# A graph network's edge rows: scattered to turns with one two-block row each, gathered once in the score pass, second blocks at the end of the last pass

## The reference, cut to what matters

```python
def _L0_gnn_ref(h, src, dst, W1, b1, W2, b2, eps):      # 3 layers
    for l in range(3):
        agg = segment_sum(h[src], dst, n)
        z = (1.0 + eps[l]) * h + agg
        h = maximum(z @ W1[l] + b1[l], 0.0) @ W2[l] + b2[l]
    return h
def _L1_gnn_ref(h, w, a, src, dst):
    hi, hj = h[src], h[dst]
    e = leaky_relu(concatenate([hi, hj], -1) @ w, 0.2) @ a
    exp_e = exp(e)
    att = exp_e / segment_sum(exp_e, src, N)[src]
    return segment_sum(hi * att, dst, N)
x = layernorm(x + _L0_gnn_ref(x, ...))
x = layernorm(x + _L1_gnn_ref(x, ...))
```

## Time and profile before

| what | value |
|---|---|
| time, median of 3 | 11068.61 us (11064.67 to 11077.53) |
| span of the profiled execution, first to last instruction | 9426.8 us |
| its own time beyond the span | not given by the page |
| POOL / PE / DVE / ACT busy | 7036.3 / 6946.3 / 5337.9 / 4916.2 us |
| layer 0, 78 to 2016 us | 1938 us |
| score stage, first gather to the last pass's first load | 2123.37 us |
| last pass, to its last turn | 1068.02 us |

### The profile page before, as it was taken

One profiled execution on the slowest core, in us unless ns is written; L12 is line 12 of the kernel. 1 busy time (PEld: TensorE's weight loads), 2 busy tenths in 40 slices (PEclk: granted clock), 3 DMA queues, 4 the chain that ended last, 5 costly groups with the idle time before them and its releaser, 6 DMA issues.

```text
span 9426.8 us, 148122 instructions
## 1 busy us (share of the span) xinstructions
PE 6946.3 (74%) x27727; PEld 4824.0 (51%) x27728; DVE 5337.9 (57%) x18200; ACT 4916.2 (52%) x11010; POOL 7036.3 (75%) x7500
## 2 busy tenths in 40 slices
PE   6777777777777777777777777777767777777776
PEld 4444444444444444444444444566667667666665
DVE  4444444444444444444444444567777777778888
ACT  5555555555555555565555555422222222267777
POOL 6777777767777777767777777667777777778886
PEclk7666666676666666676656666778887787889998
DMA  3222222232222222222222222366666666645554
GB/s 93 53 53 53 53 53 53 53 78 53 53 53 53 53 53 53 53 75 53 53 53 53 53 53 53 91 173 182 182 180 181 182 181 181 182 136 139 140 140 133
DMA packets 937711, 898.45 MB, mean 95 GB/s; under 512 B 258861, under 2 KB 778726, under 8 KB 937635
## 3 DMA queue, kind: packets, MB, share of 16 engines
q0 software_dynamic: 244544, 529.59, 21.8%
q1 hardware_dynamic: 627697, 265.87, 10.1%
q10 hardware_dynamic: 65426, 102.51, 4.0%
HBM read 751.91 MB, written 143.82 MB: 95 GB/s over the span
## 4 chain that ended last, share of the span: by engine, by line
POOL 63%; issue 23%; DVE 7%; PE 2%; ACT 2%; DVEq 1%; POOLq 1%; DMA 1%; ACTq 0%; SPq 0%
POOL rows L755 54%; POOL work L755 6%; DVE agg L1549 4%; POOL hot L755 2%; DVE big L1783 2%; ACT hot L1035 1%; PE psum L1291 1%; PE psum L1166 0%; POOLq L767 0%; ACT work L1072 0%; POOLq L459 0%; DVEq L1783 0%; PE psum L1180 0%; PE psum L1158 0%; PE psum L1189 0%
## 5 line engine op out<-in xcount | busy, mean ns | idle before, releaser
L1158 PE MATMUL psum<-work,rows 128*128 128x256 f32 x9408 | 4306.2, 607 | 1522.8 <-DMA rows<-table_g,idx_now 1000.8
L1563 DVE TENSOR_TENSOR agg<-agg,psum 128x128 f32 x9408 | 2703.0, 287 | 3152.6 <-PE psum L1158 2840.1
L1158 PEld LDWEIGHTS psum<-work,rows 128*128 128x128 f32 x9408 | 2504.6, 293 | 3323.5 <-issue 1204.5
L755 POOL DMA_INDIRECT rows<-table_g,idx_now x3136 | 2968.9, 947 | 1022.1 <-issue 1021.2
L920 ACT ACTIVATE work<-big,one_col 128x1024 f32<-128x1024 f32 x1176 | 1348.3, 1147 | 2354.3 <-PE psum L1158 2351.3
L912 ACT ACTIVATE big<-iota_w,rel_now 128x256 f32<-128x256 f32 x4704 | 1971.6, 495 | 51.9
L755 POOL DMA_INDIRECT rows<-in_x,idx_now x1568 | 1483.0, 946 | 523.3 <-issue 523.3
L996 ACT ACTIVATE work<-psum 128x256 f32<-128x256 f32 x832 | 320.7, 385 | 1456.5 <-PE psum L1256 1445.1
L755 POOL DMA_INDIRECT rows<-table_p,idx_now x832 | 803.3, 966 | 265.9 <-issue 265.3
L1291 PE MATMUL psum<-rows,hot 128*128 128x128 f32 x3328 | 658.8, 326 | 228.3 <-ACT hot L1035 201.2
L1252 PE MATMUL psum<-big,work 128*128 x3328 | 778.5, 321 | 47.4 <-ACT work L997 33.3
(11 more groups left out here) (194 smaller groups left out, 5447.2 us busy)
## 6 DMA issues: line engine op xcount, KB each, us to landing
rows<-x_of SPq DMA_DIRECT2D x416, 256.0 KB, 2.9
work<-rel_rows ACTq DMA_DIRECT2D x208, 256.0 KB
x_of<-rows SPq DMA_DIRECT2D x208, 256.0 KB, 4.2
rows<-table_g,idx_now POOLq DMA_INDIRECT x3136, 2.5
x_of<-work SPq DMA_DIRECT2D x156, 256.0 KB
big<-lo_rows ACTq DMA_DIRECT2D x208, 192.0 KB
rows<-in_x,idx_now POOLq DMA_INDIRECT x1568, 2.5
rows<-table_p,idx_now POOLq DMA_INDIRECT x832
```

The source lines that it names most:

```text
L755: pool.indirect_dma_start(out=to, out_offset=None, in_=table, in_offset=bass.IndirectOffsetOnAxis(ap=idx_now[:, at:at + 1], axis=0)) \
L1158: ins = pe.matmul(sums_at(q, t % QUAD), ring[:, t, :], span_hot[q][:, t % QUAD, :], start=True, stop=True)
L1563: dve.tensor_tensor(to, to, sums_at(q, j)[:, k * P:(k + 1) * P], ALU.add).then_inc(added[a], 1)
```

## The change

The layers' rows, in the order in which they are, are now written to new places instead of being read again. After layer 0, POOL scatters the prologue's `src` rows (`placed_src`) and relative-`dst` rows with both block numbers (`placed_rel`) to DRAM, 26 indirect DMAs with indices `place_i`, which a rank of the two-block rows gives: each turn's first place takes one two-block row, the other 15 places take one-block rows. SP loads them back, and DVE and PE go on as before. The score pass then has 98 turns (`T2` = 1568 rows) rather than 104: each row is gathered once, and the first row of a turn gets a second matmul for its second block (`hot_second`, made by DVE from the same `rel_row`). The last pass still has 104 turns: the first 1564 (`REAL`) rows, then the second blocks of the turns' first rows, whose features SP reads from `x1_of` a second time, at every 16th row.

```diff
@@ gpsimd @@
-            def gather_edges(table, to, landed):
+            def place_rows(table, of):
                 for r in range(RG):
-                    pool.indirect_dma_start(out=to[:, r, :], out_offset=None, in_=table,
-                                            in_offset=bass.IndirectOffsetOnAxis(ap=row_i[:, r:r + 1], axis=0)) \
-                        .then_inc(landed, 16)
+                    pool.indirect_dma_start(out=table, out_offset=bass.IndirectOffsetOnAxis(ap=place_i[:, r:r + 1], axis=0),
+                                            in_=of[:, r, :], in_offset=None).then_inc(rows_placed, 16)
...
-                with pool.Fori(0, LAPS if no == LAYER_A else LAPS2) as i:
+                with pool.Fori(0, LAPS2) as i:
...
@@ sync, after layer 0's tables @@
+            sp.wait_ge(rows_placed, 2 * 16 * RG)
+            sp.dma_start(g_srcf, placed_src.rearrange("(r p) e -> p r e", p=P)).then_inc(src_in, 16)
+            sp.dma_start(g_relw, placed_rel.rearrange("(r p) e -> p r e", p=P)).then_inc(dst_in, 16)
...
+            sp.dma_start(lo_all.rearrange("(r p) e -> p r e", p=P), g_lo16).then_inc(lo_out, 16)
+            sp.wait_ge(lo_out, 16)
+            sp.dma_start(lo_rows[0:REAL, :], lo_all[0:REAL, :]).then_inc(lo_out, 16)
+            sp.dma_start(lo_rows[REAL:T, :], lo_all[0:SECONDS * TPI, :].rearrange("(k s) e -> k s e", s=TPI)[:, 0, :]).then_inc(lo_out, 16)
@@ sync, last pass @@
+            def load_seconds(at, first, n):
+                sp.dma_start(slots[:, at:at + n, 0:D],
+                             x1_of[first * TPI:(first + n) * TPI, :, :].rearrange("(k s) e d -> e k s d", s=TPI)[:, :, 0, :]) \
+                    .then_inc(x1_in[at // QUAD], 16)
...
@@ tensor @@
-            for r in range(RG):
-                ins = pe.matmul(ps[0][:, 0:WINS], ones[:, :], below[:, r, :], start=(r == 0), stop=(r == RG - 1))
+            pe.matmul(ps[0][:, 0:RG], before, splits[:, 0:RG], start=True, stop=False)
+            for r in range(1, RG):
+                pe.matmul(ps[0][:, r:RG], ones, splits[:, 0:RG - r], start=False, stop=(r == RG - 1))
...
                     windows = load_windows(turn * TPI + h * HALF, PE_E)
+                    if h == 0:
+                        second = load_windows(turn + REAL, PE_E, 1)
...
+                            if t == 0:
+                                pe.matmul(sums, hot_second[:, :], q_rows[:, ds(second[0] * PW, PW)], start=False, stop=False)
...
-            with pe.Fori(0, T // RING) as i:
+            with pe.Fori(0, RINGS2) as i:
@@ vector @@
-                dve.tensor_copy(g_srcf, g_src).then_inc(g_ready, 1)
...
-                own.add(dve.tensor_tensor(g_rel, g_dst, tile_wv[:, :].rearrange("p (r o) -> p r o", o=1).to_broadcast([P, RG, P]), ALU.subtract))
...
+                if d == 0:
+                    dve.tensor_scalar(hot_second[:, :], rel_row[:, 0, 0:P], node_2[:, 0:1], None, ALU.is_equal)
                 dve.tensor_scalar(hot_t[:, d, :], rel_row[:, d // 2, (d % 2) * QUAD * P:(d % 2 + 1) * QUAD * P],
                                   node_c[:, 0:1], None, ALU.is_equal).then_inc(hot_t_ready, 1)
...
+            own.add(dve.tensor_scalar(rel_t[:, REAL:REAL + SPLITS], firsts(rel_t), -float(P), None, ALU.add))
             dve.wait_ge(rows_used, USED + FIRST_B)
+            own.add(dve.tensor_copy(src_t[:, REAL:REAL + SPLITS], firsts(src_t)))
...
+            own.add(dve.tensor_copy(exp_both[:, :, REAL:REAL + SPLITS],
+                                    exp_both[:, :, 0:SPLITS * TPI].rearrange("p b (k s) -> p b k s", s=TPI)[:, :, :, 0]))
+            own.add(dve.memset(exp_both[:, :, REAL + SPLITS:T], 0.0))
```

More of the change, by code:

```diff
@@ L613, in release, with keep_lap @@
                 sp.sem_inc(free, 1)
-            def keep_lap(lap, more):
-                for lane in range(AHEAD):
+            def keep_lap(lap, lanes, staged_lanes):
+                for lane in range(lanes):
                     for q in range(2 * lane, 2 * lane + 2):
                         keep_quad(lap, q)
-                        if q % 2 == 1 and more:
+                        if q % 2 == 1 and lane < staged_lanes:
                             stage(src_t, lane, (lap + 1) * AHEAD + lane)
@@ L689, in _ @@
                     load_quad(q, i + 1)
+            for turn in range(whole, TURNS):
+                for q in range(QUADS):
+                    sp.wait_ge(rows_used, USED + FIRST_B + (turn - 1) * TPI + (q + 1) * QUAD)
+                    first = turn * TPI + q * QUAD - REAL
+                    if first < 0:
+                        load_quad(q, turn)
+                    elif first + QUAD <= SPLITS:
+                        load_seconds(q * QUAD, first, QUAD)
+                    else:
+                        n = SPLITS - first
+                        load_seconds(q * QUAD, first, n)
+                        load_seconds(q * QUAD + n, first, QUAD - n)
             for b in range(BLOCKS):
@@ L1277, in look_up, with sum_half @@
                 ins.then_inc(looked_up, 1)
-            def sum_half(turn, h):
+            def sum_half(turn, h, last=False):
                 group = 2 * turn + h
@@ L1289, in sum_half @@
                     if j % QUAD == 0:
-                        pe.wait_ge(x1_in[2 * h + j // QUAD], 16 * (turn + 1))
+                        q = 2 * h + j // QUAD
+                        pe.wait_ge(x1_in[q], 16 * (turn + 1) + (16 if last and q == QUADS - 1 else 0))
                     pe.matmul(ps[j // 2][:, (j % 2) * D:(j % 2 + 1) * D], hot[:, j, :], row_of(h * HALF + j, D),
@@ L1461, in _ @@
                     dve.wait_ge(mix_kept, 32 * (t + 1))
-                    own.leave(T2)
+                    own.leave(REAL)
                 dve.wait_ge(e_in, 96 + 64)
@@ L1493, in _ @@
             dve.tensor_scalar(eps1[:, :], eps1[:, :], 1.0, None, ALU.add).then_inc(ones_set, 1)
-            dve.wait_ge(last_in, 16)
-            own.add(dve.tensor_copy(last_f[:, :], last_i[:, :]))
+            own.add(dve.tensor_tensor(splits[:, 0:RG], win_first[:, :], win_last[:, :], ALU.not_equal))
             own.wait()
-            for r in range(RG):
-                ins = dve.tensor_scalar(below[:, r, :], first_f[:, :], last_f[:, r:r + 1], None, ALU.is_gt)
-            ins.then_inc(counted, 1)
+            dve.reduce_sum(splits[:, RG:RG + 1], splits[:, 0:RG], axis=AX).then_inc(splits_ready, 1)
             for h in range(2):
@@ new lines, in _ @@
+            step(dve.tensor_reduce(turn_of, begun[:, :, :], axis=AX, op=ALU.add))
+            step(dve.scalar_tensor_tensor(place_f, plain, 1.0, turn_of, ALU.add, ALU.add))
+            step(dve.tensor_scalar(more, plain, all_splits, -float(PLAIN), ALU.add, ALU.add))
+            step(dve.scalar_tensor_tensor(more, more, float(TPI), place_f, ALU.mult, ALU.subtract))
+            step(dve.scalar_tensor_tensor(more, plain, float(PLAIN), more, ALU.is_ge, ALU.mult))
+            step(dve.tensor_tensor(place_f, place_f, more, ALU.add))
```

247 lines of the change are left out of this document (137 added, 110 removed).

## The result

The changed kernel takes 10,926.22 us (median of 4 runs, 10,923.18 to 10,936.96), the kernel before, run beside it, 11,073.07 us: a ratio of 0.987, 95% interval 0.9858 to 0.9882. The forecast was 10,927 us.

What follows compares the result with a forecast made beforehand. POOL's back-to-back gathers were taken to pace the layers and score stage. 9426.8 - 122.1 + 0.3 + 0.9 = 9305.9 us of span, times 1.174 = 10,927 us; range 10,890 to 10,968.

Steps and rivals of the forecast that it cites:

- The gain is six turns of the score pass: Score stage: 1568 gathers instead of 1664, 96 x 1.2718 = 122.1 us less; other engines' work hidden.
- an even stretch: Whole program: a timed run is the profiled one stretched by 1.174, giving 10,927 us; chance 0.58 with everything hidden.
- The 1641.8 us as a fixed part outside the span: Rival, whole run: the time beyond the span stays fixed, so 9305.9 + 1641.8 = 10,948 us; chance 0.20.
- POOL paces the score stage: Score stage: POOL's gathers, back to back at 1.2718 us a step, set the pace; POOL waits for almost nobody.
- Second blocks hidden: Score stage, 98 times: about 1.2 us more on PE and a compare on DVE, within 5.6 us free; cost nothing.
- `hot_second` holds POOL: Rival, score stage: each compare blocks POOL, 13 to 52 us of span, 10,942 to 10,988 us; 0.10 shared with 3 us scatters.
- Scatters cost what the reads do on POOL: Between layer 0 and 1: 26 scatters at the reads' price, 1.25 us each; nothing lost up to 2.2 us each.
- the dear scatters: Rival, between layer 0 and 1: at 8 us a scatter, 11,100 us; slower 0.03. At 3 us, 10,960; 0.10 shared.
- 25.53 us of cover: Between layer 0 and 1: POOL's 25.53 us wait for the tables behind its 26 reads, taken to hide scatter cost.
- PE becomes the pace: Rival, score stage: PE needs 5.6 us more per turn to match POOL, 1.2 found; time then about as before.
- Last pass and end of the score stage: Last pass: still 104 turns, 1068 us, costs nothing; after the score stage, three small VectorE copies, +0.9 us.
- prologue: Ahead of layer 0: work changes off POOL's path, except two copies ahead of the staged indices, +0.3 us.

Runs made afterwards that it cites:

- doubled scatters: The changed kernel with the 26 scatters issued twice, the first time to arrays that nothing reads: 11,036.76 us, 0.9889 of the kernel before.
- the first profile: First profile of the kernel before, unchanged, on which the prediction was built: span 9426.8 us, beside timed runs of 11,068.6 us.
- the threefold matmul: The changed kernel with the second block's compare and matmul each made three times: 11,008.69 us, 0.9864 of the kernel before.
- the second profile: The kernel before, profiled again with no edit: 11,164.47 us, with a span of 11,162.6 us.

## Why the prediction was right, point by point

- **The gain is six turns of the score pass: right.** On one chip the stage's gathers went from 2622.94 to 2468.86 us, 154.1 us, and no other stage but the doubled scatters' moved by over 2 us.
- **The size of that term: 122.1 us of span times 1.174 is 143; measured 154.** The factor rested on an even stretch, and the stretch was not even: 1.240 in the score stage, 1.000 in the last pass. With the stage's own factor the term is 122.1 x 1.240 = 151.4. That the median came within 1 us of the forecast is luck. The forecast took 142 us off the 11,068.6 of three runs; the gain was 11,073.07 - 10,926.22 = 146.9 us, and the kernel before, with a fourth run, came out 4.5 us higher.
- **The 1641.8 us as a fixed part outside the span: fell, as the chances had it.** Times and spans lie 1.7 to 1.9 us apart in both profiles that went like a timed run. A span of 9306, expected as the sign of being right, did not come for the same reason; the score stage's 2001 us neither.
- **POOL paces the score stage: half right.** Half the gathers take 8.2 us off the turn, so their number matters to it. But the step "back to back, waiting for nobody" was read from the first profile: in a timed run POOL waits 5.4 us of a turn's 25.2 for SP. The prediction named such waits as a sign that PE or DVE had become too long; they are there in the kernel before as well, so here they say nothing of the change. The layers are not back to back either: POOL's pauses there, 3.8 us each, make them 1.18 to 1.20 times as long. The sum survived because its factor came from whole runs, so that it took in the pauses with the steps.
- **Second blocks hidden: right**, and the sizes too: 0.47 us for the matmul (forecast 0.48 to 0.64 and a load), 0.44 us for the compare (0.13 to 0.53, though "near 0.2" was expected; the 128x512 one beside it takes 0.54, so a quarter of the columns is not a quarter of the time).
- **`hot_second` holds POOL: fell.** Gathers of the score stage take 0.971 and 0.976 us into two of the buffers in the changed kernel and 0.970 and 0.977 in the kernel before, both profiled in a run like the timed ones, and with three compares a turn the turn is 0.05 us longer than with none.
- **Scatters cost what the reads do on POOL: right** (0.97 us against 0.95), so the dear scatters fell. **That 25.53 us of cover hide them: wrong**, without harm to the sum, since 26 reads stood in their place. Doubling their 33 us cost 24 us in that stretch, and 28 to 32 us in all.
- **PE becomes the pace: fell** with the threefold matmul.
- **Last pass and end of the score stage: right; prologue: not to be told.** The last pass takes 1068.03 us against 1067.48. Between the stage and the first fetch are 49.97 us against 48.57, +1.4 where +0.9 was forecast. POOL's first gather comes at 48.03 against 48.82, where +0.3 was forecast, and between 48.0 and 50.6 in the runs of the changed kernel and its variants.

## What to carry to other kernels

When a profile's span and the timed runs differ by 17%, the profile shows another execution: profile again before sharing the difference out, and look which stages it is in. Price work by the stage as it is timed: a whole turn taken away was worth 154.1 / 6 = 25.7 us here, not only POOL's own steps in it (20.35), while gathers alone, left out of a turn, were worth 1.03 us each, less than POOL's step of 1.27. And an idle stretch behind a burst of such DMAs is no proof that the burst is free: double the burst and see whether the end of the stretch moves.

## What the runs showed of the hardware

**In timed runs a long burst of POOL's indirect DMAs held up VectorE, ScalarE and TensorE.** While gathers or scatters followed each other at 1.25 to 1.32 us without a pause, VectorE's additions went from 0.32 to 1.40 us apart, the tables' steps from 1.75 to as much as 12.7 us. In the score stage ACT stood still for up to 14.2 us with no releaser in the trace, and TensorE for up to 7.5 us. In the layers and behind them the hold-up set in some 10 to 13 us after POOL's last pause, and it ended in the next pause or some microseconds behind the burst. An addition's own duration stays 287 ns, so the time is lost ahead of it and not in it. The Trainium skill (SBUF — State Buffer, Who interferes with whom) has VectorE and GpSimd exclude each other at a shared port pair, and PE and ACT outside it. No run here shows that lock at work in the score stage, and what is seen reaches PE, ACT and VectorE alike.

**Bytes are not what it goes by.** The same rows in 13 scatters of 1032 bytes a partition held the tables up 13.4 us less than in 26 of 512 and 520. The 13 are also half as many pieces to write, so whether it goes by instructions, by pieces or by the length of the burst is not shown.

**What stays open.** It is open what the other engines lack while POOL issues, and why the first profile of the kernel before had none of it. There the same gathers of 0.946 us ran beside additions of 8 in 2.54 us, at a granted clock of 0.707 against 0.754 in the second, so it was not a faster TensorE. The Trainium skill (Runtime: NRT & Kernel Launch, Instruction fetch mechanics) says that an engine's sequencer fetches its instructions in blocks by a DMA queue of its own, and that a taken branch to a target outside the two blocks at hand stalls it. The tables' steps are straight code and were held up too, so no branch is needed for it. The page of the kernel before shows two queues of that kind, with the same packets in both profiles:

```profile
q8 instruction: 15, 0.25, 0.0%
q14 instruction: 29, 0.24, 0.0%
```

From 200 to 2300 us of the second profile, in layer 0 and its hold-ups, neither queue has a packet. So fetches on these two queues are not what the additions wait for; fetches that the profile does not record are not excluded.
